# KV product at step 20, Y at 21 to 24, and the low halves of turned tiles on both sides of the gate

## What is computed

```
qkv = x @ Wqkv + bqkv;  q, k, v = split(qkv)
q = q - mean(q);  k = k - mean(k)                      # over channels
q2 = l2norm(q*q / sum(q*q), axis=channels)
k2 = l2norm(k*k / sum(k*k), axis=tokens)
kv = einsum('bnc,bnd->bcd', k2, v)
x  = layernorm(x + (v + q2 @ kv / sqrt(N)) @ Wln + bln)
sel    = sigmoid(x @ expert_sel.T)                     # 16 experts
scores = relu(einsum('bsd,edh->bseh', x, keys))
x  = layernorm(x + einsum('bseh,ehv,bse->bsv', scores, values, sel))
```

## Time and profile before

| | |
|---|---|
| median of 3 runs | 1028.7 us (1028.34 to 1030.61) |
| the profiled execution | 1027.94 us |
| its span, first to last instruction | 1026.1 us |
| mean granted TensorE clock | 0.993 |
| TensorE busy | 995.9 us, 97% |
| VectorE busy | 815.5 us, 79% |
| ScalarE busy | 528.7 us, 52% |
| GpSimd busy | 213.9 us, 21% |

### The profile page before, as it was taken

The page is one execution under the profiler, slowest core; times in us unless marked ns, Lnnn a source line. Parts: engine busy times, 40 slices in busy tenths (PEclk is TensorE's granted clock), DMA queues, the critical chain, the costliest instruction groups (busy, mean ns, idle before and its releaser), DMA issues.

```text
span 1026.1 us, 22008 instructions
## 1 busy us (share of the span) xinstructions
PE 995.9 (97%) x8324; PEld 979.6 (95%) x8324; DVE 815.5 (79%) x1874; ACT 528.7 (52%) x1150; POOL 213.9 (21%) x267
## 2 busy tenths in 40 slices
PE   7899999999999999999999999999999999999996
PEld 6799999999999999999999999999999999999996
DVE  5789887888868888688877889778887889867565
ACT  4566554465445654456544565356554466444332
POOL 0021212212221222212222112221221222122221
PEclk8999999999999999999999999999999999999999
DMA  5031111211122011220121210212111211110100
GB/s 183 22 121 66 44 63 42 86 62 43 63 84 83 21 44 66 80 101 25 32 77 61 103 43 31 75 63 85 43 63 42 85 63 43 63 43 33 33 22 21
DMA packets 47982, 62.20 MB, mean 61 GB/s; under 512 B 4098, under 2 KB 34562, under 8 KB 47876
## 3 DMA queue, kind: packets, MB, share of 16 engines
q1 hardware_dynamic: 47876, 60.79, 17.4%
HBM read 37.18 MB, written 23.07 MB: 59 GB/s over the span
## 4 chain that ended last, share of the span: by engine, by line
PE 77%; DVE 13%; ACT 5%; issue 4%; DMA 0%; DVEq 0%; POOL 0%; ACTq 0%; POOLq 0%
PE down_bank L1324 27%; PE up_bank L1324 27%; PE ring_bank L1324 8%; PE qk_bank L1324 7%; PE g_bank L1324 3%; DVE gated L1088 3%; DVE gated_l L1094 2%; ACT gated_h L553 2%; DVE qT_l L946 2%; ACT z L635 1%; DVE x1T_l L952 1%; PE ring_bank L1575 1%; PE ring_bank L1576 1%; PE g_bank L1370 1%; DVE z L990 1%
## 5 line engine op out<-in xcount | busy, mean ns | idle before, releaser
L539 POOL PARTITION_BROADCAST sel_all<-sel_rows x240 | 199.4, 831 | 680.3 <-DVE gated L1088 641.7
L553 ACT ACTIVATE gated_h<-gated 128x512 fp32r<-128x512 f32 x256 | 161.6, 631 | 303.2 <-DVE gated L1088 301.3
L1324 PE MATMUL down_bank<-vals_h,gated_h 128*128 128x256 f32 x1024 | 288.8, 282 | 5.8 <-DVE gated_l L1094 4.2
L1324 PE MATMUL up_bank<-x1T_h,keys_h 128*128 128x256 f32 x1024 | 285.4, 279 | 0.0
L1324 PE MATMUL up_bank<-x1T_l,keys_h 128*128 128x256 f32 x1024 | 285.3, 279 | 0.0
L1324 PE MATMUL up_bank<-x1T_h,keys_l 128*128 128x256 f32 x1024 | 285.3, 279 | 0.0
L1324 PE MATMUL down_bank<-vals_l,gated_h 128*128 128x256 f32 x1024 | 285.0, 278 | 0.0
L1324 PE MATMUL down_bank<-vals_h,gated_l 128*128 128x256 f32 x1024 | 285.0, 278 | 0.0
L1094 DVE TENSOR_TENSOR gated_l<-gated,gated_h 128x512 fp32r<-128x512 f32 x256 | 171.8, 671 | 51.6 <-ACT gated_h L553 49.9
L1088 DVE SCALAR_TENSOR_TENSOR gated<-up_bank,sel_all 128x512 f32<-128x512 f32 x256 | 176.1, 688 | 44.1 <-PE up_bank L1324 41.5
L1324 PEld LDWEIGHTS down_bank<-vals_h,gated_h 128*128 128x128 f32 x1024 | 192.6, 188 | 11.8 <-DVE gated_l L1094 6.7
(11 more groups left out here) (252 smaller groups left out, 1699.2 us busy)
## 6 DMA issues: line engine op xcount, KB each, us to landing
out<-z SPq DMA_DIRECT2D x32, 256.0 KB, 2.4
x_raw<-in_x SPq DMA_DIRECT2D x15, 512.0 KB, 4.8
xT_raw<-in_xT SPq DMA_DIRECT2D x14, 512.0 KB, 4.1
parked_q<-w_room SPq DMA_DIRECT2D x14, 512.0 KB, 3.0
q<-parked_q SPq DMA_DIRECT2D x56, 128.0 KB, 3.0
parked_x<-w_room SPq DMA_DIRECT2D x14, 512.0 KB, 2.6
z<-parked_x SPq DMA_DIRECT2D x56, 128.0 KB, 3.0
w_room<-in_keys SPq DMA_DIRECT2D x4, 512.0 KB, 3.4
```

The costliest lines, as they stand in the source:

```text
L539: nc.gpsimd.partition_broadcast(sel_all[:, e % 2], row, P).then_inc(sel_spread, 1)
L553: return nc.scalar.activation(dst, src, ACT.Copy, **kw)
L1324: last = mm(dst, lhs, rhs, start=start and i == 0, stop=stop and i == n - 1, **kw)
```

## The change

- The plan: KV goes from step 21 to 20, Y 0 to 3 from 22 to 25 to 21 to 24 (XS with them), Y 4 and 5 from 2 and 4 to 1 and 3, ZN of the first group from 19 and 20 to 25 and 26, QR 0 from 20 to 18, XR 0 from 29 to 28, QS to later steps (11 to 20, so far 9 to 20).
- QR and XR: the subtraction for the first half stays in `early(s + 1)`, ahead of the gate; that for the second goes to the start of `late(s + 1)`, behind it.
- The x bias goes from ahead of the gate to behind it, for pairs 2 and 3 from steps 27 and 28 to 30 and 31.
- `add_zs` goes ahead of `split_lo`.
- Turned x1 lands in `w_room` and not in `z`. The waits of z and of SP that protected z go; the transposes wait for the low halves in their place.

```diff
 LOOP = dict(
     plan={
-        1: [("ZA", 0), ("ZA", 1)], 2: [("ZN", 0), ("Y", 4)], 3: [("ZN", 1), ("XS", 4)], 4: [("Y", 5)],
+        1: [("ZA", 0), ("ZA", 1), ("Y", 4)], 2: [("ZN", 0), ("XS", 4)], 3: [("ZN", 1), ("Y", 5)], 4: [],
         5: [("Y", 6), ("XS", 5)], 6: [("Y", 7), ("XS", 6)], 7: [("XS", 7), ("QK", 0)], 8: [("QK", 1)],
-        9: [("GG", 0), ("QS", 0)], 10: [("XR", 1), ("QK", 2), ("GG", 1), ("QS", 1)], 11: [("QK", 3), ("LG", 1)],
-        12: [("GG", 2), ("QK", 4), ("QS", 2)], 13: [("GG", 3), ("QS", 3)], 14: [("QK", 5)],
-        15: [("GG", 4), ("QK", 6)],
-        16: [("GG", 5), ("QS", 4)], 17: [("ZA", 0), ("ZA", 1), ("QK", 7)],
-        18: [("GG", 6), ("QS", 5)], 19: [("KS", 0), ("ZN", 0), ("GG", 7), ("QS", 6)],
-        20: [("QR", 0), ("ZN", 1), ("QS", 7)], 21: [("KV", 0)], 22: [("Y", 0)], 23: [("Y", 1), ("XS", 0)], 24: [("Y", 2), ("XS", 1)],
-        25: [("Y", 3), ("XS", 2)], 26: [("XS", 3)], 27: [("QR", 1)], 29: [("XR", 0)], 30: [("LG", 0)],
+        9: [("GG", 0)], 10: [("XR", 1), ("QK", 2), ("GG", 1)], 11: [("QK", 3), ("LG", 1), ("QS", 0)],
+        12: [("GG", 2), ("QK", 4), ("QS", 1)], 13: [("GG", 3), ("QS", 2)], 14: [("QK", 5), ("QS", 3)],
+        15: [("GG", 4), ("QK", 6), ("QS", 4)], 16: [("GG", 5), ("QS", 5)], 17: [("ZA", 0), ("ZA", 1), ("QK", 7)],
+        18: [("QR", 0), ("GG", 6)], 19: [("KS", 0), ("GG", 7), ("QS", 6)], 20: [("KV", 0), ("QS", 7)],
+        21: [("Y", 0)], 22: [("Y", 1), ("XS", 0)], 23: [("Y", 2), ("XS", 1)], 24: [("Y", 3), ("XS", 2)],
+        25: [("XS", 3), ("ZN", 0)], 26: [("ZN", 1)], 27: [("QR", 1)], 28: [("XR", 0)], 30: [("LG", 0)],
     },
-    bias_x={9: 0, 14: 1, 27: 2, 28: 3},
+    bias_x={9: 0, 14: 1, 30: 2, 31: 3},
...
-    10: [("XT", 7), ("QK", 2), ("GG", 1), ("QS", 0)], 11: [("QK", 3), ("QS", 1)],
-    12: [("GG", 2), ("QK", 4), ("LG", 1), ("QS", 2)]}
+    10: [("XT", 7), ("QK", 2), ("GG", 1)], 11: [("QK", 3), ("QS", 0)],
+    12: [("GG", 2), ("QK", 4), ("LG", 1), ("QS", 1)]}
...
-        turned_x = z[:].rearrange("p a t c -> p (a t c)")
+        turned_x = w_room[:]
...
-                else:
-                    for p in range(2):
-                        at_least(sp, stored[p], 16 * (2 * it + 1 - h))
...
+            def x_low(b, g, m):
+                dve.wait_ge(x1T_hi, tile(b, GT * g + 2 * m + 1))
+                at_m = lambda part: quarters(part[:, g, m].rearrange("p (a n) -> p a n", a=GT))
+                V.tensor_tensor(at_m(x1T_l), by_tile(turned_x, m), at_m(x1T_h).bitcast(F32),
+                                ALU.subtract).then_inc(x1T_lo, 2)
...
-                    if 0 < it < B:
-                        dve.wait_ge(x1T_lo, tile(it, T - 1) if off == 0 else tile(it, GT - 1))
...
             def late(it, s):
+                for kind, a, off in planned(it, s - 1, ("QR", "XR")):
+                    (q_low if kind == "QR" else x_low)(it + off, a, 1)
+                add_x_bias(it, s)
                 add_qk_bias(it, s)
...
+                elif kind == "QS" and a < GT:
+                    dve.wait_ge(x1T_lo, tile(b - 1, T - 1))
+                elif kind == "XS" and a >= GT:
+                    dve.wait_ge(x1T_lo, tile(b, GT - 1))
...
                 early(it, s)
+                add_zs(it, s)
                 split_lo(it, s)
-                add_zs(it, s)
```

More of the change, by code:

```diff
@@ L840, in split_lo, with add_x_bias @@
                     V.tensor_tensor(x_l[:], pair_x, x_h[:].bitcast(F32), ALU.subtract).then_inc(x_lo, 1)
+            def add_x_bias(it, s):
+                sch = schedule(it)
                 if s in sch["bias_x"] and has(it, 1):
@@ L942, in early @@
                     elif kind == "QR":
[L943 to L947, removed]
-                    elif kind == "XR":
[L949 to L953, removed]
+                        q_low(b, a, 0)
+                    elif kind == "XR":
+                        x_low(b, a, 0)
                     elif kind == "XT":
@@ L972, in early, with q_low @@
                                        z_rstd[:, a, 1:2]).then_inc(last_out_made, 1)
+            def q_low(b, h, m):
+                dve.wait_ge(qT_hi, q_pair(b, 2 * h + m))
+                at_m = lambda part: quarters(part[:].rearrange("p u v m n -> p (u v) m n")[:, :, m])
+                V.tensor_tensor(at_m(qT_l), by_tile(turned_q[h], m), at_m(qT_h).bitcast(F32),
+                                ALU.subtract).then_inc(qT_lo, 1)
+            def x_low(b, g, m):
[3 more added lines that the diff above has]
+                                ALU.subtract).then_inc(x1T_lo, 2)
             def add_zs(it, s):
```

## The result

The changed kernel takes 1021.41 us (median of 4, 1020.76 to 1022.37); the kernel before took 1029.65 beside it (4 runs, 1028.34 to 1031.21). The ratio is 0.9918, with a 95% interval of 0.9897 to 0.9938: faster by 0.8%, 8.2 us. The profiled execution took 1022.37 us, its span is 1020.6, that is 5.5 less than before.

The account below looks back on a forecast made before the run. TensorE, busy 97%, was taken as the bound, through its waits and matmul pitch. Against 1027.94 us, -14.4 + 7.6 + 4.6 + 2.1 + 0.5 = +0.4; forecast 1028.7, no change, range 1021.5 to 1034.5.

Parts of the forecast that it names:

- (a): Step 22: the Y product's wait for kvw_l goes, with 0.3 us of room; 5.0 us gained.
- (e): First batch, step 12: a Gram product's wait for k_l shrinks as a q transpose leaves step 10; 0.4 us gained.
- (b): Step 30: the logits' wait for the low half of turned x1 goes; 4.8 us gained.
- (f): Step 11: group 1's logits newly wait for the half behind the gate, 1.15 us in six batches; 7.6 us lost.
- (g): Step 20: KV newly waits for g's low half, 0.65 us in each of seven batches; 4.6 us lost.
- (h): Step 29: the down product still waits for gated_l, 0.3 us longer in each of seven batches; 2.1 us lost.
- (i): Turned x leaving z's room, waits on z and SP: nothing; 0.5 us added for small waits at steps 4, 16, 17.
- Rival 2: Steps 11, 19, 28, 29: the broadcast takes the ports from halves behind the gate; slower, 1034.8 us; chance 0.15.
- Rival 4: Y product of step 21: kvw_l still ends a wait, 5 us not gained; 1033.7 us; chance 0.02.
- Rival 1: New waits in steps 11, 20 and 29 are small, so faster: 1021.6 us; chance 0.25.
- Rival 3: TensorE's matmul pitch alone moves the time by more than 3 us, to 1024 or 1033 us; chance 0.08.
- (c): Step 1: Y of tile 4 between up and down removes the down product's wait for z; 2.3 us gained.

Follow-up runs that it names:

- Rows first: Changed kernel with SP moving group 1's weight rows ahead of the turn of q in step 14: 1018.0 us, ratio 0.9882 to the kernel before.
- q copies first: Changed kernel with x1's group 1 second half in front of the gate, and ScalarE copying turned q ahead of the z passes: 1011.3 us.
- Y 4 at step 2: Changed kernel with Y of tiles 4 and 5 and tile 4's transpose back in steps 2, 4 and 3: 1030.4 us, ratio 1.0006 to before.
- ZN at 4: Changed kernel, x1's group 1 half in front of the gate, second z normalisation in step 4, not 3: 1007.8 us; with q copies first added, 1005.8.
- half behind gated_l: Changed kernel with x1's group 1 second half in front of the gate and q's group 1 second half behind gated_l: 1017.3 us.

## Why the prediction was right and wrong

- **(a) to (e), the waits taken away**: right, to 0.2 us each. Reading them start to start gave 14.4; the table says 14.8. The view of waits alone would have given 7.3 for (a) and (b) and not the 10.2 that were there.
- **(f)**: right in mechanism; 1.35 each and not 1.15. I had 1.18 for a fast batch; the gate comes 0.08 later behind the step's start than before, and the matmul behind the wait is late by another 0.09 (712.22 to 712.54, where 0.23 is the pitch), which I had counted in steps 22, 29 and 30 but not here. 8.8 in all.
- **(g)**: this is the step that failed, 4.6 forecast and 0.15 there. The ten links were right: from the start of gated_h of step 18 to the end of g's low half I had 5.1, and it takes 5.1 (744.29 to 749.38). What was wrong is when the chain starts. I kept both meetings of steps 15 and 16 with a broadcast, 0.4 each, added 0.36 for a transpose, and so had the gate of step 17 at up to S17 + 3.7; it comes at + 2.8 to 3.3, since the weight rows are issued 2.3 to 4.4 us later, counted from S17, and most meetings go. "Rows first" brings back one of them in every batch, and with it 0.20 of wait at the fast pitch; a second one would make that some 0.6, which was my 0.65 (an estimate, no run has both). The pitch does the rest: five batches that (f) turns slow want KV 0.35 later. I had followed the change on VectorE and past SP's stores, but had not asked what the turn of q, one step later and still ahead of the rows on SP, does to the time of a broadcast. That KV doesn't wait is also what I had named as a sign of being wrong.
- **(h)**: right in kind; 0.2 each and not 0.3, so +1.3 and not +2.1. The gate of 28 came at S28 + 2.46, as worked out. The stretched broadcast gives 0.27 of step 29's 0.87 (I had 0.3 for it); with the q copies first on ScalarE nothing of the 0.87 is left. A count in it was off by one: 29 of the 56 k_l are slowed, not 30.
- **(i)**: no large wait came of it. Small stalls moved (0.08 new in step 25, 0.1 less in step 26) and became 0.7 less in all, where I had 0.5 more.
- **Rival 2** fell: gated_l is held for 0.28, not 0.7. **Rival 4** fell. **Rival 1** was the nearest: it named (g) as the term on which it rests, and its 1021.6 stands beside 1021.4. That close is luck in part: its small (g) was right, its small (f) wrong by 2.9, and 2.7 of the measured gain is the step from the profiled executions to the medians.
- **Rival 3**, the pitch: between the two profiled executions it moved nothing (45% and 44%). Yet it is not noise as I treated it: "Y 4 at step 2" and "ZN at 4" show it tied to single stalls. (c) is worth 2.4 by its waits, yet taking it back takes back all of the gain in the median.
- **From span to median**: forecast and measured lie 7.3 apart, 1028.7 and 1021.4. Of these 5.6 are in the table, and (g) is 4.45 of them. The profiled executions differ by 5.5, the medians by 8.2. The profiled one of before was its fastest, that of after its slowest. What lies in the other executions no trace shows; that they differ in the pitch would fit, but is not shown.

## What to carry to other kernels

A step moved on a DMA queue moves whatever is queued behind it, and through it the moment when another engine starts: ask that of every queue before costing a chain at its ends. A new place for an instruction is worth trying one use at a time: of the four halves put behind the gate, x1's of group 1 cost 8.8 us, q's of group 0 gave KV its room, q's of group 1 saved 0.3 a batch, net of the 0.27 that it costs through the broadcast, and for x1's of group 0 no run tells. And where a moved piece pays, find out which of its companions pays: here KV one step earlier is a loss by itself. A rerun that is to bring back the old state has to be held against the old trace: "rows first" put the rows where they had never been.

## What the runs showed that I had not expected

TensorE has two steady pitches for the same matmul (256 columns, its weights loaded beside the one before): 113.3 or 117.7 ns, at a granted clock of 1.00 in either. A stretch keeps its pitch for up to some 850 matmuls. With few exceptions it goes over only where the stream is interrupted, be it by 0.05 us, or where matmuls of another width stand in it. Which way it goes depends on the place. Behind the eight 2-column matmuls of KS (step 19) 85 of the 98 batches in the 14 traces were slow. KV has 256 columns as well; most of its twelve matmuls follow at 120 ns, and behind them all 98 batches were slow, eight of which had come to it fast and turned without a gap. The 0.08 us stall of step 25 turned all seven batches of the changed kernel fast again, six of seven when that kernel ran again, and three of seven in "half behind gated_l". At steps 4 and 11 it went either way. The difference, 4.4 ns, is 4.4 us per thousand matmuls; over the runs here the slow share ranged from 0.29 to 0.53, 8 us of the launch. So taking away a stall can be worth several times its length (ZN at 4: 0.4 at the stall, 2.9 by the pitch) or nothing (q copies first: 5.1 saved, 3.5 given back). What in the engine sets the pitch stays open.
